# Single-tile node loads in a ring of eight, and more gathered rows fetched by SyncE and ScalarE

## The chip, the cores and the metric

The kernel runs on one core of a Trainium2 chip. The metric is the device time of one execution in microseconds (us); several executions are made and their median is given. The engines are PE (TensorE), DVE (VectorE), ACT (ScalarE), POOL (GpSimd) and SP (SyncE, which only issues transfers here). All run at the same time and wait for each other by semaphores. ACT and SP also have a queue of their own for transfers (ACTq and SPq in the rows).

## The reference

One layer of a graph network over N = 12,500 nodes with D = 256 features and E = 200,000 edges. The edges are sorted by their destination.

```python
h = jnp.maximum(_layernorm(x, axis=-1), 0.0)
agg = jax.ops.segment_sum(h[src], dst, num_segments=N)
z = (1.0 + eps_gin) * h + agg
t = jax.nn.relu(_batchnorm(jnp.dot(z, W1) + b1, g1, bt1))
conv_out = jnp.dot(t, W2) + b2
out = x + jax.nn.relu(_batchnorm(conv_out + h, g2, bt2))
```

The batch norms are over all nodes, so nothing behind the first one can start before t is known for every node.

## The kernel before

**Tiles, groups, windows.** The edges are cut into 1563 tiles of 128. A tile is gathered as 128 rows of 1 KB, one on each partition. Eight tiles make a group; there are 196 groups (the last has three tiles). All edges of a group fall into a window of 96 destination nodes. For each group DVE writes a 0/1 selection matrix, PE multiplies it with the gathered rows (`aggregate`, line 1324, two recorded matmuls a tile), ACT or DVE copies the result out of PSUM (`keep_window`, line 1151, or line 918), PE transposes it (line 1334) and DVE adds it into `aggT` (line 840).

**The x part and the h part.** For groups 0 to 29 the rows of x are gathered, and DVE and ACT compute the layer norm on the gathered rows (`statistics` line 676, `normalise` line 1103). In the same time ACT and DVE normalise the whole of x once, in 25 batches, and store it to HBM as `h_rows`. From group `H_FROM = 30` on the gather reads `h_rows` and no norm is needed.

**Three gatherers.** POOL issues one indirect DMA for a tile (line 650). It takes the groups in order, and a group g waits until group g - 4 has been aggregated (`s_agg`). Some tiles are left out of POOL's list. The last tile of each group in `sp_groups` is fetched by SP, the last but one of each group in `act_groups` by ACT, row by row, each row a DMA of 1 KB whose address comes from a register (lines 512 and 1197). Addresses are brought in as a line of 128 from the HBM table `row_at` (lines 492 and 1178) and read into registers 32 at a time (`reg_load`). Each of the two has three places for tiles (`ROW_BUFS`), so its j-th tile waits for the aggregation of its tile j - 3.

**The pace of SP and ACT.** SP's program goes over passes c = 0 to 97, one for each tile of 128 nodes, thus one pass for two groups. `SP_EIGHTHS` is the number of pieces of 16 rows that it fetches in eight passes: 12, which is 24 rows a pass. ACT's program goes by groups; `ACT_EIGHTHS = 7` is 14 rows a group, from group `H_ACT = 29` on. The lists come out as follows: SP has 16 tiles (two of the x part, groups 16 and 26, and 14 of the h part), ACT has 17 (groups 42 to 188).

**Node tiles.** PE also needs each node tile of h itself, to transpose it (`transpose_h`, line 1351); tile c is transposed in PE's step 2c + 7, where aggregate(g) belongs to step g + 1. The first `H_NODES = 14` are loaded from x and normalised (lines 460 and 1137). The other 84 are loaded from `h_rows` in `quads` of four (line 467), with two quads of space. Quad k >= 2 waits until every tile of quad k - 2 has been transposed, and SP waits there, in the pass with (c - 14) % 4 == 2:

```python
if k >= 2:
    sp.wait_ge(s_hT, H_NODES + QUAD * (k - 1))
```

In every fourth pass SP also stores t to HBM (`store_t`, line 476), for which it waits until four `t` blocks have been made. That is about step 2c.

**ACT around the change of parts.** Up to step 32 ACT's program has, in one step, the norm of the last group, the square roots, then the rows of the step, and behind them `keep_hT`, `keep_window(g - 2)`, `norm_node_tile` and `t_and_b1`. From step 33 on it holds only row fetches until step 191; DVE does the copies.

**The end.** After the last group PE finishes `t`, the first batch norm follows, then the W2 matmuls (line 1442), the second batch norm and the output (line 1456).

Of the kernel before, what the change touches and what calls it, by code (L numbers as in the profile page):

```python
# [20 lines left out]
P = 128  # L21
D = 256
F = 512
DB, FB = D // P, F // P
GT = 8
# [11 lines left out]
XW = Q * D  # L37
X_FIRST = 4
X_EARLY = 16
SP_EIGHTHS = 12  # L40
ACT_EIGHTHS = 7
H_FROM = 30
H_NODES = 14
HB = 4
# [4 lines left out]
ROW_BUFS = 3  # L49
PIECE = 16  # L50
AT_ONCE = 32
QUAD = 4
ROW_BYTES = 4 * D


def ceil(a, b):
    return -(-a // b)


def build(nc, x, src, dst, W1, b1, g1, bt1, W2, b2, g2, bt2, eps_gin, out):  # L60
# [4 lines left out]
    N, E = x.shape[0], src.shape[0]  # L65

    NI = ceil(E, P * SLOTS)
    NT = ceil(N, P)
    assert NI == NT and NI >= 4 and N % 4 == 0 and NI * PG <= BANK
    LASTN = N - P * (NT - 1)  # L70
# [15 lines left out]
    with ctx:  # L86
# [3 lines left out]
        def sem(name):  # L90
            return ctx.enter_context(nc.semaphore(name))
# [4 lines left out]
        h_dram = nc.dram_tensor("h_rows", (N, D), f32, kind="Internal").ap()  # L96
# [3 lines left out]
        def eighths(q, n):  # L100
            return q * n // 8
# [3 lines left out]
        while True:  # L105
            done = ceil(8 * per_tile * (len(sp_groups) + 1), SP_EIGHTHS)
            if done > H_NODES or 2 * (done - 1) + 6 >= H_FROM:
# [3 lines left out]
        while True:  # L111
            done = ceil(8 * per_tile * (len(sp_groups) - SP_X + 1), SP_EIGHTHS) + H_NODES
            if 2 * (done - 1) + 6 >= NG - 4:
# [4 lines left out]
        while True:  # L118
            done = ceil(8 * per_tile * (len(act_groups) + 1), ACT_EIGHTHS) + H_ACT
            if done - 1 + 4 >= NG - 4:  # L120
# [22 lines left out]
        work, once, tables, ring = (arena[:, sum(MAIN[:n]):sum(MAIN[:n + 1])] for n in range(4))  # L143
# [6 lines left out]
                 work[:, 2 * GT * D:3 * GT * D])]  # L150
        hb = [a[:, n * 4 * D:(n + 1) * 4 * D].rearrange("p (j d) -> p j d", d=D) for a in
              (ring[:, 2 * GT * D:3 * GT * D], work[:, 2 * GT * D:3 * GT * D]) for n in (0, 1)]
        quads = [ring[:, 2 * GT * D + n * QUAD * D:2 * GT * D + (n + 1) * QUAD * D].rearrange("p (j d) -> p j d", d=D)
                 for n in (0, 1)]
        assert (NT - H_NODES) % QUAD == 0 and 2 * QUAD == GT
        after_rows = [work[:, 3 * GT * D + n * D:3 * GT * D + (n + 1) * D] for n in range(4)]
        tab_i = [work[:, n * EB * P:(n + 1) * EB * P].bitcast(i32).rearrange("p (b e) -> p b e", e=P) for n in (0, 1)]
        tab_f = [work[:, (2 + n) * EB * P:(3 + n) * EB * P].rearrange("p (b e) -> p b e", e=P) for n in (0, 1)]
# [42 lines left out]
        hx = after_rows[3]  # L201
# [68 lines left out]
        s_bn, s_mv, s_sd, s_rstd, s_st, s_h, s_sel, s_agg, s_add = (  # L270
            sem(n) for n in ("s_bn", "s_mv", "s_sd", "s_rstd", "s_st", "s_h", "s_sel", "s_agg", "s_add"))
        s_xt = [sem("s_xt_even"), sem("s_xt_odd")]
        s_quad = [sem("s_quad_even"), sem("s_quad_odd")]
        s_ev, s_wT = sem("s_ev"), sem("s_wT")
        s_xbn, s_xmv, s_xsd, s_xrs, s_xst, s_hx, s_hT, s_hTc, s_zt, s_t, s_tb, s_tst, s_td = (
            sem(n) for n in ("s_xbn", "s_xmv", "s_xsd", "s_xrs", "s_xst", "s_hx", "s_hT", "s_hTc", "s_zt",
                             "s_t", "s_tb", "s_tst", "s_td"))
# [50 lines left out]
        def row_pieces(first, end, tiles):  # L328

            return [divmod(n, P // PIECE) for n in range(first, min(end, tiles * P // PIECE))]  # L330
# [13 lines left out]
        def batch_nodes(a, b, first, end):  # L344

            return a[b * QN + 4 * first:b * QN + 4 * end, :].rearrange("(p j) d -> p j d", j=4)

        NQUAD = (NT - H_NODES) // QUAD

        def quad_count(k):  # L350

            return 16 * (k // 2 + 1 + (k == NQUAD - 1))

        def quad_tile(c):

            k, j = divmod(c - H_NODES, QUAD)
            return quads[k % 2][:, j, :]

        def wait_h(eng):

            for b in range(NQ - HB, NQ):
                wait_apart(eng, s_hd[b % HB], batch_count(b))
# [49 lines left out]
        def last_order(i):  # L412

            return (NQF, TAILN // 4) if i == 0 else (i - 1, P)
# [13 lines left out]
        def _(sp):  # L428
# [17 lines left out]
            for a in (b1, g1, bt1, b2, g2, bt2):  # L446
                k = a.shape[0] // P
# [7 lines left out]
            def load_node_tile(c, n=P):  # L455
                if c == 1:
                    sp.wait_ge(s_add, 1)
                if c >= 2:
                    sp.wait_ge(s_hx, c - 1)
                sp.dma_start(xt[c % 2][0:n, :], x[bass.ds(c * P, n), :]).then_inc(s_xt[c % 2], 16)  # L460

            def load_quad(k):
                if k >= 2:
                    sp.wait_ge(s_hT, H_NODES + QUAD * (k - 1))
                first = H_NODES + QUAD * k
                n = QUAD if k < NQUAD - 1 else QUAD - 1
                sp.dma_start(quads[k % 2][:, 0:n, :],
                             h_dram[first * P:(first + n) * P, :].rearrange("(j p) d -> p j d", p=P)
                             ).then_inc(s_quad[k % 2], 16)
                if n < QUAD:  # L470
                    sp.dma_start(quad_tile(NT - 1)[0:LASTN, :], h_dram[N - LASTN:N, :]).then_inc(s_quad[k % 2], 16)

            def store_t(q):
                sp.wait_ge(s_tb, FB * (q + 1))
                if q < NQF:
                    sp.dma_start(t_dram[q, :, :, :], tb[:, :, :]).then_inc(s_td if q < NQF - 1 else s_td_full, 16)
                else:
                    sp.dma_start(t_dram[q, :, :, 0:TAILN], tb_last[:, :, :]).then_inc(s_td_tail, 16)
# [11 lines left out]
            def load_at(j):  # L490
                b, p = divmod(sp_groups[j] * GT + GT - 1, P)
                sp.dma_start(sp_at[j % 2], at_dram[b, p:p + 1, :]).then_inc(s_spat[j % 2], 16)
# [26 lines left out]
            def pieces_of_pass(c):  # L519

                if c < H_NODES:
                    return row_pieces(eighths(SP_EIGHTHS, c), eighths(SP_EIGHTHS, c + 1), SP_X)
                c -= H_NODES
                return [(SP_X + j, m) for j, m in row_pieces(eighths(SP_EIGHTHS, c), eighths(SP_EIGHTHS, c + 1),
                                                            len(sp_groups) - SP_X)]

            def load_t(q, k, r, n=QN):
                if at_least(q, 2):
                    sp.wait_ge(s_u, FB * (q - 1))
                sp.dma_start(tin[:, k % 2, :, 0:n],  # L530
                             t_dram[bass.ds(q, 1), :, :, 0:n].rearrange("c p f n -> p (c f) n")
                             ).then_inc(s_tin[k % 2], 16)
# [3 lines left out]
            for c in range(NT):  # L536
                if c == NT - 1:
                    store_t(NQF - 2)
                if c < H_NODES:
                    load_node_tile(c)  # L540
                elif c == H_NODES:
                    wait_h(sp)
                    load_quad(0)
                    load_quad(1)
                elif (c - H_NODES) % QUAD == 2 and (c - H_NODES) // QUAD + 2 < NQUAD + 1:
                    k = (c - H_NODES) // QUAD + 1
                    if k >= 2:
                        load_quad(k)
                if 2 * Q < c < NT - 1 and c % Q == 1:
                    q = (c - 2 * Q - 1) // Q  # L550
                    if q == NQF - 3:
                        sp.wait_ge(s_td, 16 * q)
                        load_t(0, 0, 0)
                    store_t(q)
                if c == 0:
                    sp.wait_ge(s_trc[0], NTR)
                    sp.wait_ge(s_trc[1], NTR)
                    for b in (2, 3):
                        sp.dma_start(hb[b], batch_nodes(x, b, 0, P)).then_inc(s_pl[b], 16)
                    sp.wait_ge(s_atd, 16)  # L560
                    load_at(0)
                for j, m in pieces_of_pass(c):
                    load_rows(j, m)
# [47 lines left out]
            q, n = last_order(NQ - 1)  # L611
# [455 lines left out]
        def _(act):  # L1067
# [136 lines left out]
            def step(g):  # L1204
# [10 lines left out]
                if g >= H_ACT:  # L1215
                    for j, m in row_pieces(eighths(ACT_EIGHTHS, g - H_ACT), eighths(ACT_EIGHTHS, g - H_ACT + 1),
                                           len(act_groups)):
# [72 lines left out]
        def _(pe):  # L1290
# [46 lines left out]
            def transpose_h(c):  # L1337
                n = P if c < NT - 1 else LASTN
                if c < H_NODES:
                    pe.wait_ge(s_hx, c + 1)  # L1340
                else:
                    k = (c - H_NODES) // QUAD
                    pe.wait_ge(s_quad[k % 2], quad_count(k))
                h = hx if c < H_NODES else quad_tile(c)
                if 1 <= c < NT - 1:
                    pe.wait_ge(s_hTc, c)
                if c == NT - 1:
                    pe.wait_ge(s_sel, NG)
                hT = hT_ps if c < NT - 1 else hT_last
                for f in range(DB):  # L1350
                    last = T.transpose(hT[:, f, 0:n], h[0:n, f * P:(f + 1) * P], ident[0:n, 0:n])
                last.then_inc(s_hT, 1)
# [40 lines left out]
            a, c, q = NG - 4, NT - 4, NQF - 2  # L1393
# [90 lines left out]
```

## Time and profile before

| | |
|---|---|
| time, median of 3 runs | 2143.56 us (2143.31 to 2145.06) |
| the profiled execution: time, span | 2143.43 us, 2141.6 us |
| POOL: busy, and indirect DMAs | 1449.2 us (68%), 1530 of them from 3.8 to 1916.5 us |
| PE busy | 1430.6 us (67%) |
| DVE busy, ACT busy | 768.3 us (36%), 338.3 us (16%) |
| rows fetched one by one: SP, ACT | 2048, 2176 |
| HBM read, written | 271.55 MB, 52.05 MB |

The span is from the first to the last recorded instruction. Busy leaves out instructions that only issue a DMA from SP or ACT, register loads and waits. The share of PE is that of pipelined matmuls and is no measure of how near PE is to its limit.

### The profile page before, as it was taken

The numbers are of one execution on the slowest core, as the hardware profiler recorded it, in microseconds if no ns is written. First come the engines' busy times: TensorE is split into PE (matmuls) and PEld (weight loads), VectorE is DVE, ScalarE is ACT, GpSimd is POOL, SyncE is SP. The second block draws the span as 40 slices with busy tenths as digits, with TensorE's granted clock in tenths as the row PEclk, the third lists the DMA queues.
The fourth block names the chain that finished last, engine by engine and source line by source line (L and its number), as shares of the span: only waits on it lengthen the run. The fifth ranks groups of instructions, "written<-read, shape, count | busy, mean of one in ns | idle before, by whom it ended". The sixth has DMA issues, their size and how long they took to land.

```text
span 2141.6 us, 24025 instructions
## 1 busy us (share of the span) xinstructions
PE 1430.6 (67%) x4835; PEld 911.2 (43%) x4835; DVE 768.3 (36%) x1947; ACT 338.3 (16%) x661; POOL 1449.2 (68%) x1540
## 2 busy tenths in 40 slices
PE   3656666665655766675666566666666666689998
PEld 2434344443433434343444334434344444454446
DVE  7777753222322222322232222222232232234447
ACT  6767660000000000000000000000000000014446
POOL 7777777777777777777777777777777777760000
PEclk7788788877888787888888887778787788899999
DMA  6666654444434434444444443443443444448438
GB/s 200 214 224 218 225 175 129 132 117 139 138 108 139 138 110 136 137 118 130 136 126 119 138 139 108 138 137 107 140 137 108 136 135 123 137 133 321 176 135 319
DMA packets 123554, 325.22 MB, mean 152 GB/s; under 512 B 32179, under 2 KB 55294, under 8 KB 117266
## 3 DMA queue, kind: packets, MB, share of 16 engines
q0 software_dynamic: 73440, 200.64, 32.0%
q1 hardware_dynamic: 39100, 97.34, 12.8%
q10 hardware_dynamic: 10870, 25.75, 3.6%
q8 instruction: 38, 0.62, 0.1%
q14 instruction: 106, 0.87, 0.1%
HBM read 271.55 MB, written 52.05 MB: 151 GB/s over the span
## 4 chain that ended last, share of the span: by engine, by line
POOL 65%; issue 21%; PE 12%; DMA 2%; ACT 0%; DVE 0%; SPq 0%; POOLq 0%; DVEq 0%
POOL arena L650 65%; PE ps L1442 8%; PE ps L1324 2%; PE ps L1456 2%; DMA arena<-h_rows,arena 1%; PE ps L1360 0%; PE ps L1398 0%; DMA arena<-in_src 0%; ACT aggT L1072 0%; SPq L439 0%; ACT arena L1078 0%; ACT arena L1076 0%; DVE arena L1057 0%; PE ps L1334 0%; SPq L433 0%
## 5 line engine op out<-in xcount | busy, mean ns | idle before, releaser
L650 POOL DMA_INDIRECT arena<-h_rows,arena x1292 | 1221.6, 946 | 394.0 <-issue 391.5
L1324 PE MATMUL ps<-arena 128*96 128x256 f32 x3060 | 976.9, 489 | 675.2 <-DMA arena<-h_rows,arena 561.5
L1324 PEld LDWEIGHTS ps<-arena 128*96 128x96 f32 x3060 | 640.8, 216 | 993.3 <-issue 732.4
L840 DVE TENSOR_TENSOR aggT<-aggT,ps 128x192 f32 x196 | 69.3, 353 | 1074.2 <-PE ps L1334 1071.2
L1151 ACT COPY arena<-ps 96x256 f32<-96x256 f32 x37 | 13.2, 357 | 1575.5 <-PE ps L1334 1545.0
L650 POOL DMA_INDIRECT arena<-in_x,arena x222 | 209.9, 946 | 67.7 <-issue 67.7
L1360 PE MATMUL ps<-arena 128*128 128x512 f32 (+3 forms) x412 | 186.3, 577 | 1.6 <-DVE arena L873 1.5
L1442 PE MATMUL ps<-arena,W2s 128*128 128x512 f32 (+1 forms) x400 | 168.1, 582 | 0.9 <-ACT arena L1272 0.8
L927 DVE TENSOR_TENSOR arena<-arena,ps 128x768 f32<-128x768 f32 x159 | 149.8, 942 | 0.0
L1103 ACT ACTIVATE arena<-arena,nb,mv 128x256 f32<-128x256 f32 x238 | 120.2, 587 | 83.6 <-DVE nb L744 81.5
L1442 PEld LDWEIGHTS ps<-arena,W2s 128*128 128x128 f32 x400 | 75.7, 190 | 93.2 <-issue 86.3
L676 DVE BATCH_NORM_STATS2 st<-arena 128x6 f32<-128x256 f32 x238 | 80.5, 410 | 61.5 <-DMA arena<-in_x,arena 61.4
L1360 PEld LDWEIGHTS ps<-arena 128*128 128x128 f32 x412 | 69.7, 190 | 48.1 <-issue 44.5
L1272 ACT ACTIVATE arena<-arena,sh,sc 128x512 f32<-128x512 f32 (+1 forms) x100 | 72.1, 792 | 90.2 <-PE ps L1442 80.3
L924 DVE TENSOR_SCALAR arena<-ps,prmT 128x512 f32<-128x512 f32 x79 | 59.3, 751 | 73.7 <-PE ps L1360 73.7
L1035 DVE SCALAR_TENSOR_TENSOR aggT<-ps,prmT,aggT 128x512 f32<-128x512 f32 (+1 forms) x50 | 36.9, 738 | 95.7 <-PE ps L1442 95.7
L881 DVE BATCH_NORM_STATS2 arena<-arena 128x6 f32<-128x512 f32 x92 | 62.9, 684 | 10.3 <-ACT arena L1160 10.3
L1334 PEld LDWEIGHTS ps<-ident,arena 96*128 96x128 f32 x392 | 55.3, 142 | 26.5 <-ACT arena L1151 1.2
L918 DVE COPY arena<-ps 96x256 f32<-96x256 f32 x159 | 65.8, 414 | 0.1
L1334 PE MATMUL ps<-ident,arena 96*128 96x96 f32 x392 | 64.9, 246 | 0.6 <-ACT arena L1151 0.5
L1117 ACT ACTIVATE arena<-arena,pnb,pmv 128x256 f32<-128x256 f32 (+1 forms) x100 | 51.7, 591 | 0.0
L756 DVE TENSOR_TENSOR arena<-arena,ps 128x768 f32<-128x768 f32 x37 | 35.0, 945 | 8.7 <-PE ps L1324 8.7
(99 smaller groups left out, 575.2 us busy)
## 6 DMA issues: line engine op xcount, KB each, us to landing
W2s<-h_rows ACTq DMA_DIRECT2D x2176, 1.0 KB
rl_odd<-h_rows SPq DMA_DIRECT2D x1792, 1.0 KB
t_T<-arena SPq DMA_DIRECT2D x24, 1024.0 KB, 4.9
arena<-t_T SPq DMA_DIRECT2D x24, 1024.0 KB, 4.8
arena<-h_rows,arena POOLq DMA_INDIRECT x1292, 2.8
arena<-in_x SPq DMA_DIRECT2D x27, 512.0 KB, 5.7
h_rows<-arena ACTq DMA_DIRECT2D x24, 512.0 KB, 3.4
out<-arena SPq DMA_DIRECT2D x23, 512.0 KB
```

The costliest lines, as they stand in the source:

```text
L650: nc.gpsimd.indirect_dma_start(out=rows[slot(g)][:, k, :], out_offset=None, in_=(x if g < H_FROM else h_dram)[:, :], in_offset=bass.Indire ...
L676: last = V.bn_stats(o, r)
L840: V.tensor_tensor(z, z, winT_ps, ALU.add).then_inc(s_add, 1)
L881: V.bn_stats(o, t[:, m, :]).then_inc(s_tst, 1)
L918: V.tensor_copy(win_sb[g % 2], win_ps[g % 2]).then_inc(s_ev, 1)
L927: V.tensor_tensor(sel[:, g % 2, :, :], rel[:, g * GT:(g + 1) * GT].unsqueeze(2).to_broadcast([P, GT, W]), iota_ps.unsqueeze(1).to_broadcas ...
L1103: last = S.activation(rows_of(g, k), rows_of(g, k), ACT.Relu, bias=nb[:, g % 2, k:k + 1], scale=mv[:, g % 2, k, 1:2])
L1272: S.activation(u[:, k % 2, f, 0:n], tin[:, k % 2, f, 0:n], ACT.Relu, bias=sh1[:, f:f + 1], scale=sc1[:, f:f + 1]).then_inc(s_u, 1)
L1324: last = T.matmul(win_ps[g % 2], sel[:, g % 2, k, :], rows_of(g, k), start=k == 0, stop=k == n - 1)
L1334: last = T.transpose(winT_ps[:, f, :], win_sb[w % 2][:, f * P:(f + 1) * P], ident[0:W, 0:W])
L1360: last = T.matmul(t_ps[(FB * q + m) % TB][:, a:b], W1s[:, k, m * P:(m + 1) * P], zt[q % 2][:, k, a:b], start=k == 0, stop=k == DB - 1)
L1442: last = T.matmul(c_ps[k % 2][m][:, 0:n], W2s[:, f, m * P:(m + 1) * P], u[:, k % 2, f, 0:n], start=f == 0, stop=f == FB - 1)
```

## The change

The node tiles of the h part are loaded one at a time into a ring of eight places with a semaphore each, in the same memory as the two quads. Four are loaded at pass 14; each later pass c loads tile c + 3, and waits for the transpose of tile c - 5 (`s_hT >= c - 4`). The constants `SP_EIGHTHS` and `ACT_EIGHTHS` go from 12 to 22 and from 7 to 11: 44 rows a pass for SP, 22 a group for ACT. The lists then are: SP 31 tiles (four of the x part, groups 10, 16, 22 and 28, and 27 of the h part), ACT 27 tiles (groups 38 to 190). In 17 groups both fetch a tile (before: in two). The last group of either is 190.

```diff
-SP_EIGHTHS = 12
-ACT_EIGHTHS = 7
+SP_EIGHTHS = 22
+ACT_EIGHTHS = 11
...
-QUAD = 4
+NODE_BUFS = 8
+NODES_AHEAD = 4
...
-            def load_quad(k):
-                if k >= 2:
-                    sp.wait_ge(s_hT, H_NODES + QUAD * (k - 1))
-                first = H_NODES + QUAD * k
-                n = QUAD if k < NQUAD - 1 else QUAD - 1
-                sp.dma_start(quads[k % 2][:, 0:n, :],
-                             h_dram[first * P:(first + n) * P, :].rearrange("(j p) d -> p j d", p=P)
-                             ).then_inc(s_quad[k % 2], 16)
-                if n < QUAD:
-                    sp.dma_start(quad_tile(NT - 1)[0:LASTN, :], h_dram[N - LASTN:N, :]).then_inc(s_quad[k % 2], 16)
+            def load_node_rows(c):
+                n = P if c < NT - 1 else LASTN
+                if c - NODE_BUFS >= H_NODES:
+                    sp.wait_ge(s_hT, c - NODE_BUFS + 1)
+                sp.dma_start(node_tile(c)[0:n, :], h_dram[c * P:c * P + n, :]
+                             ).then_inc(s_node[(c - H_NODES) % NODE_BUFS], 16)
...
                 elif c == H_NODES:
                     wait_h(sp)
-                    load_quad(0)
-                    load_quad(1)
-                elif (c - H_NODES) % QUAD == 2 and (c - H_NODES) // QUAD + 2 < NQUAD + 1:
-                    k = (c - H_NODES) // QUAD + 1
-                    if k >= 2:
-                        load_quad(k)
+                    for n in range(NODES_AHEAD):
+                        load_node_rows(c + n)
+                elif c + NODES_AHEAD - 1 < NT:
+                    load_node_rows(c + NODES_AHEAD - 1)
...
                 else:
-                    k = (c - H_NODES) // QUAD
-                    pe.wait_ge(s_quad[k % 2], quad_count(k))
-                h = hx if c < H_NODES else quad_tile(c)
+                    pe.wait_ge(s_node[(c - H_NODES) % NODE_BUFS], node_count(c))
+                h = hx if c < H_NODES else node_tile(c)
```

## Rows read from the trace of the kernel before

**Rows 1.** The page: busy time of each engine, and 40 slices of POOL

```profile
PE 1430.6 (67%) x4835; PEld 911.2 (43%) x4835; DVE 768.3 (36%) x1947; ACT 338.3 (16%) x661; POOL 1449.2 (68%) x1540
...
POOL 7777777777777777777777777777777777760000
```

**Rows 2.** The page: the chain that ended last, by engine

```profile
POOL 65%; issue 21%; PE 12%; DMA 2%; ACT 0%; DVE 0%; SPq 0%; POOLq 0%; DVEq 0%
```

**Rows 3.** Line 650, POOL's gathers: durations (ns), first and last start, idle time before them

```profile
L650 POOL DMA_INDIRECT arena<-h_rows,arena x1292: 942/946/1005, 302.2 to 1916.5; - x185
L650 POOL DMA_INDIRECT arena<-in_x,arena x222: 942/946/969, 24.6 to 300.9; - x111
...
  issue: 463.7, 1521
  PE ps L1324: 2.4, 8
```

**Rows 4.** Windows of line 650: POOL busy (count), PE's granted clock, DMA share, GB/s

```profile
770.00:800.00 30.00, 22.69 (x25) 0.83 0.37 107
1052.00:1082.00 30.00, 22.69 (x25) 0.83 0.40 116
```

**Rows 5.** Waits: PE's aggregation for gathers (total us, times, longest)

```profile
PE ps L1324 <- DMA arena<-h_rows,arena: 561.5, 150, 7.9
```

**Rows 6.** Timeline of ACT's queue: start us, us

```profile
530.73 0.27 ACTq L1178 DMA_DIRECT2D W2s<-row_at  x1
533.36 51.78 ACTq L1197 DMA_DIRECT2D W2s<-h_rows  x128
585.18 0.27 ACTq L1178 DMA_DIRECT2D W2s<-row_at  x1
```

**Rows 7.** Timeline of SP's queue, h part

```profile
1052.30 30.99 SPq L512 DMA_DIRECT2D rl_odd<-h_rows  x80
1114.06 0.40 SPq L467 DMA_DIRECT2D arena<-h_rows  x1
1114.55 5.12 SPq L512 DMA_DIRECT2D rl_odd<-h_rows  x16
1121.81 0.36 SPq L476 DMA_DIRECT2D t_T<-arena  x1
1122.21 0.27 SPq L492 DMA_DIRECT2D rl_odd<-row_at  x1
1126.68 30.58 SPq L512 DMA_DIRECT2D rl_odd<-h_rows  x80
```

**Rows 8.** DMA queues and issues between 1170 and 1230 us (q10 is ACT's)

```profile
q10 hardware_dynamic: 174, 0.09, 0.6%
...
W2s<-h_rows ACTq DMA_DIRECT2D x83, 1.0 KB
```

**Rows 9.** x part: SP's row fetches, a node tile's issue, and DVE's reading it

```profile
61.95 14.53 SPq L512 DMA_DIRECT2D rl_odd<-in_x  x32
...
97.32 11.87 SPq L512 DMA_DIRECT2D rl_odd<-in_x  x32
114.77 0.37 SPq L460 DMA_DIRECT2D arena<-in_x  x1
...
139.70 0.41 DVE L676 BATCH_NORM_STATS2 xst<-arena 128x6 f32<-128x256 f32 x1
```

**Rows 10.** Timeline of ACT and PE at the change of parts

```profile
308.63 4.04 ACT L1103 ACTIVATE arena<-arena,nb,mv 128x256 f32<-128x256 f32 x8 [6.40 <-DVE nb L744]
...
312.68 0.35 ACT L1151 COPY arena<-ps 96x256 f32<-96x256 f32 x1
...
313.99 0.23 ACTq L1178 DMA_DIRECT2D W2s<-row_at  x1
...
316.63 0.49 ACTq L1197 DMA_DIRECT2D W2s<-h_rows  x1
...
318.15 3.67 PE L1324 MATMUL ps<-arena 128*96 128x256 f32 x16
```

More of the change, by code:

```diff
@@ L152, in build @@
               (ring[:, 2 * GT * D:3 * GT * D], work[:, 2 * GT * D:3 * GT * D]) for n in (0, 1)]
-        quads = [ring[:, 2 * GT * D + n * QUAD * D:2 * GT * D + (n + 1) * QUAD * D].rearrange("p (j d) -> p j d", d=D)
-                 for n in (0, 1)]
-        assert (NT - H_NODES) % QUAD == 0 and 2 * QUAD == GT
+        node_rows = ring[:, 2 * GT * D:3 * GT * D].rearrange("p (j d) -> p j d", d=D)
+        assert NODE_BUFS == GT
         after_rows = [work[:, 3 * GT * D + n * D:3 * GT * D + (n + 1) * D] for n in range(4)]
@@ L272, in build @@
         s_xt = [sem("s_xt_even"), sem("s_xt_odd")]
-        s_quad = [sem("s_quad_even"), sem("s_quad_odd")]
+        s_node = [sem(f"s_node{b}") for b in range(NODE_BUFS)]
         s_ev, s_wT = sem("s_ev"), sem("s_wT")
@@ L346, in batch_nodes, with node_tile, node_count @@
             return a[b * QN + 4 * first:b * QN + 4 * end, :].rearrange("(p j) d -> p j d", j=4)
[L348 to L357, printed above, removed]
+        def node_tile(c):
+            return node_rows[:, (c - H_NODES) % NODE_BUFS, :]
+        def node_count(c):
+            return 16 * ((c - H_NODES) // NODE_BUFS + 1)
         def wait_h(eng):
```

## The prediction

> **What bounds the kernel now.** I read the page first. No engine is busy above 68%, but POOL's slices stand at 7, without a dip, for nine tenths of the span [rows 1]. The chain that ended last gives POOL 65%, "issue" 21% and PE 12% [rows 2]. So I read the line of the gathers next. Each takes 946 ns. The h part's 1292 start between 302.2 and 1916.5 us, so one comes every (1916.5 - 302.2) / 1291 = 1.2504 us. The 0.304 us between two of them (463.7 / 1521) is POOL's own issue time, for it waits for PE only 2.4 us in total [rows 3]. The reader should see that a busy share of 76% here is a full engine. The waits say the same from the other side: PE waits 561.5 us for gathers in 150 places [rows 5]. From 3.8 to 1916.5 us the time is the number of POOL's gathers times 1.2504 us. Behind that lie 225 us (2141.6 - 1916.5) of PE-led work that the change doesn't touch.
>
> **What the change removes.** SP has 31 tiles instead of 16, ACT 27 instead of 17. POOL's list falls by 15 + 10 = 25 gathers, from 1530 to 1505, and 25 x 1.2504 = 31.3 us go, if nothing else becomes late. What could become late is taken in turn: the two row queues, the x part, the change of parts, PE, and the DMA engines.
>
> **ACT's queue, 22 rows a group.** A tile fetched back to back takes 54.45 us from one `row_at` load to the next (530.73 to 585.18), reads of registers and the load within it [rows 6]. In that stretch SP fetched rows as well, for a part of it. After the change a group has 8 - 44/128 = 7.656 POOL tiles, so it lasts 9.573 us, and ACT owes a tile every 128/22 = 5.82 groups, or 55.7 us. It is 98% full, but it fits. It also has a start: its first tile can be complete at about 309 + 54 = 363 us, while group 38 is gathered by POOL at about 387 us. Each tile adds 1.2 us to these 24 us. Its wait for a free place (`s_agg` of its tile three earlier) isn't reached with that lead.
>
> **SP's queue, 44 rows a pass.** SP is paced by `store_t` in every fourth pass, so I sum a round of four passes, which is eight groups or 76.6 us. It has 176 rows. Sixteen rows take 5.12 us, so a row costs 0.32 us; 80 rows take 30.58 us, so each of the two reads of 32 registers in them costs (30.58 - 25.6) / 2 = 2.5 us [rows 7]. 176 x 0.32 = 56.3; 5.5 reads x 2.5 = 13.7; the read behind the store of t takes 4.2 us (1122.48 to 1126.68), 1.7 more than the others; four node loads of 0.40 us and 0.1 us to the next issue are 2.0; the store 0.4; 1.4 loads of addresses 0.4. The sum is 74.5 us, 97% of the round. The other streams don't slow it: 80 rows took 30.99 and 30.58 us beside ACT's.
>
> The smaller node loads are paid here: four issues instead of one in a round, 3 x 0.5 = 1.5 us of the sum. The new wait on `s_hT` is for the transpose in step 2c - 3. The old one held SP until step 2c + 1 in its pass. `store_t` holds SP until step 2c, so I expect the new wait to hold nothing. So the ring by itself is worth nothing, in either direction; with the old waits a round of 74.5 us would fit as well, since they too come once in four passes. What lies behind SP's waits is its row tiles and node tiles. The last pass of a round, c + 3, ends at about step 2c + 7.6, and what it finished is used in step 2(c + 3) + 7, so 5.4 groups or 52 us are spare. Costs that SP hides fall on nobody until these are gone.
>
> **The x part.** SP has 32 pieces in the first 12 passes instead of 16 in 11. Here 32 rows take 11.87 to 14.53 us, dearer than in the h part [rows 9]; a pass of three pieces is about 20 to 22 us, against 19.6 us for two groups. SP drifts by some us, and no piece is left for passes 12 and 13. What is queued behind them is the next node tile. Before, that of pass 4 was issued at 114.77 us, and DVE read it at 139.70 us [rows 9]. From pass 1 at 61.5 us on, three passes of three pieces put pass 4 at about 128 us. With some 3 us to land that leaves 8 us, the least of all passes by this count. I take nothing for the x part; its bound is what passes each 3 us longer would cost, 1 to 2 us. Two of the 25 gathers are saved in it.
>
> **The change of parts.** In steps 29 to 32 ACT has five pieces instead of three, ahead of the window copies that PE waits for. Before, step 29 had none: norm at 308.63 us, window copy at 312.68 us; step 30 began its rows 2.6 us behind the `row_at` load at 313.99 us (316.63) [rows 10]. Everything is 2.5 us earlier by now. In step 29 the load, the read of registers and 16 rows take about 8 us from 306.2 us, of which the norm's 4.04 us cover half. So the copy slips by 4 us, and so does the aggregation that began at 318.15 us and ended at 321.8 us [rows 10]. POOL needs it for group 33, 24 gathers behind the start at 302.2 us, at 332.2 us. Its spare time falls from 10.4 to 6.4 us. In step 31 there are 32 rows and a read, 13.5 us, and the copy comes 10 us later than before. That aggregation ends at about 339 us, while POOL needs it at about 350 us. No loss; bounds are nothing, and 10 us if each of the five pieces took twice its 5.1 us and a read.
>
> **PE.** A group lasted (8 - 26/128) x 1.2504 = 9.75 us, and PE waited 561.5 / 162 = 3.5 us of it, so its own work is 6.3 us. It gets 9.57 us, and in the groups where both SP and ACT fetch a tile 7.5 us. It fits, with four groups of buffer.
>
> **The DMA engines.** No byte is added. POOL made 25 gathers in 30 us both beside ACT's rows alone and beside ACT's and SP's; the DMA share was 0.37 and 0.40 [rows 4]. The row packets themselves: ACT's queue had 0.6% of 16 engines for 60 us, 5.8 us for 83 rows, 0.07 us a row [rows 8]. In a group 44 rows are 3.1 us. If all fell on one engine, that one would be busy 0.37 x 9.57 + 3.1 = 6.6 us of 9.57 us.
>
> The Trainium skill speaks against such rows. "DMA: Bandwidth & Descriptors", section "Why a DMA increments its semaphore by 16 and not by 1", says that a transfer whose slowest dimension doesn't divide further runs on few engines, the lowest-numbered of the 16. No row here shows the engine of a packet. By that rule the sum would be the same, as long as this one engine isn't full. The section "Issuing engines are not separate DMA queues" says that issuing from several engines saves only issue time; issue time is what the gathers of rows 3 are made of, so there the trace agrees.
>
> **The sum.** 2143.43 - 31.3 = 2112.2 us against the profiled execution, 0.13 us below the median: 2112.3 us.
>
> **The rivals.**
> - *Stall at the change of parts or in the x part.* For it: both ACT and SP hold copies and node tiles behind rows there. Against it: 6 and 8 us of spare time. 2 to 10 us, thus 2114 to 2122 us. Chance 0.06.
> - *A row queue is late (the slower side).* ACT and SP have never been full together for more than 31 us. If ACT needed more than (1841.5 - 363) / 26 = 56.9 us a tile, its last one would be later than POOL's group 190 (1885.2 - 35 x 1.25 = 1841.5 us). At 58.1 us, 7% above 54.45, the 31.3 us are lost; at 60 us its last tile is 82 us late and the time about 2194 us, slower than before. SP decides from a round of 76.6 + (52 + 31) / 19.6 = 80.8 us, 8% above its sum. Against it: the tile of rows 6 and the 80 rows of rows 7 were fetched at full pace, with the other queue at work for part of the time. Chance 0.06, half of it above 2148 us.
> - *PE becomes the bound.* It would need half as much work again for each group; 2120 to 2143 us. Chance 0.03.
> - *One DMA engine fills up with rows.* From 0.138 us a row, twice the measured one, a group would last as long as that engine; at three times it would be 3.5 + 9.3 = 12.8 us, and 162 groups of the h part would add some 520 us. Chance 0.02.
> - *The forecast:* 0.83.
>
> **How the numbers follow.** The forecast's own spread is that of the three runs, 1.8 us. From 2110.5 us the range reaches over the nearer half of the stalls, to 2119 us. About 4.3 us (0.2%) is what can be told from no change. Faster: 0.83 + 0.06 + 0.03 + 0.03 less a little, 0.93; same 0.02; slower 0.05.
>
> **What would show it.** Right: line 650 has 1505 starts, 1.250 us apart, the last at about 1885 us, with PE as releaser for under 5 us in total; ACT's `row_at` loads are 54 to 55 us apart throughout; SP's round holds 176 rows in about 74 us and its line for the node load shows no wait; the part behind the last gather is still 225 us. Wrong: gaps in line 650 around 300 to 350 us with PE as releaser (first rival), or late in the h part, with PE waiting for DMA into `rl_odd` or `W2s` (second).

## The result and the profile after

The changed kernel takes 2169.32 us (median of 4 runs, 2166.32 to 2170.07) against 2143.43 us: ratio 1.0117, 95% interval 1.0099 to 1.0134. By the medians it is 25.9 us slower. The forecast was 2112.3 us, 2110.5 to 2119 us, with a chance of 0.05 for slower.

The page of the changed kernel, its busy times, POOL's 40 slices and the chain that ended last:

```profile
PE 1369.2 (63%) x4835; PEld 883.3 (41%) x4835; DVE 766.2 (35%) x1947; ACT 338.4 (16%) x661; POOL 1425.5 (66%) x1515
...
POOL 7777777777777777777767767677666777760000
...
POOL 40%; SPq 24%; issue 18%; PE 13%; DMA 5%; ACT 0%; DVE 0%; POOLq 0%; DVEq 0%
```

Beside [rows 1] and [rows 2], the reader should see two things. POOL's slices now have sixes from the middle of the h part on. And a quarter of the chain is SP's queue, which before was nowhere in it. The line of the gathers (line 641 now) answers to [rows 3]:

```profile
L641 POOL DMA_INDIRECT arena<-h_rows,arena x1269: 940/946/962, 299.8 to 1940.7; - x182
...
  issue: 453.9, 1488
  PE ps L1315: 60.2, 16
```

There are 1505 gathers in all, as forecast, and each still takes 946 ns. But POOL waited for PE for 60.2 us, and the last one starts at 1940.7 us. Counted over all steps between gathers, 56.3 us are above 1.2504 us a step (0.9 us before, near the start, and about the same there now). This excess is called POOL's loss below. The account closes: 2141.6 - 31.3 (25 gathers) + 55.4 (new stalls) + 1.9 (the part behind the last gather is 227.0 us instead of 225.1) = 2167.6, and the span is 2167.7 us. So the 31.3 us were saved, and a new wait took more than that back.

Whom PE and DVE wait for, in the changed kernel (total us, times, longest):

```profile
DVE arena L915 <- DMA t_T<-arena: 283.1, 15, 34.9
PE ps L1315 <- DMA rl_odd<-h_rows: 172.0, 14, 21.9
PE ps L1315 <- DVE arena L918: 92.0, 8, 24.0
...
POOL arena L641 <- PE ps L1315: 60.2, 16, 9.8
```

None of the first three was there before. `rl_odd` holds SP's row tiles, `t_T` is SP's store of t. Both come from SP: it is late. The third follows from the first: DVE can't write the next block of t until the store is done, the selection matrix (line 918) comes behind that, and PE needs the matrix. SP's own waits between 330 and 1860 us say so, of the kernel before and of the changed one:

```profile
SPq L467 <- PE ps L1351: 630.7, 19, 64.0
SPq L476 <- DVE arena L924: 126.5, 20, 20.2
```

```profile
SPq L498 <- PE ps L1315: 11.2, 6, 3.2
SPq L469 <- DVE arena L915: 2.7, 2, 1.6
```

Before, SP waited 757 us of 1530 us in these two lines (`store_t` and the quads' wait). Now it waits 14 us. It has next to no spare time, where the forecast had left it 3%. Its queue in one round, from a store of t to the next:

```profile
1008.09 0.42 SPq L469 DMA_DIRECT2D t_T<-arena  x1
1008.55 0.85 SPq L485 DMA_DIRECT2D rl_odd<-row_at  x1
1013.03 23.50 SPq L505 DMA_DIRECT2D rl_odd<-h_rows  x48
1036.58 0.37 SPq L463 DMA_DIRECT2D arena<-h_rows  x1
1037.04 13.56 SPq L505 DMA_DIRECT2D rl_odd<-h_rows  x32
1050.65 0.36 SPq L463 DMA_DIRECT2D arena<-h_rows  x1
1051.11 18.93 SPq L505 DMA_DIRECT2D rl_odd<-h_rows  x48
...
1073.06 21.14 SPq L505 DMA_DIRECT2D rl_odd<-h_rows  x48
1094.25 0.37 SPq L463 DMA_DIRECT2D arena<-h_rows  x1
1094.67 0.44 SPq L469 DMA_DIRECT2D t_T<-arena  x1
```

The round is 1094.67 - 1008.09 = 86.6 us for 176 rows; the mean of 15 rounds is 83.2 us. By [rows 7] 48 rows with one read of registers would be 17.9 us. Here they are 18.9 to 23.5 us. From one row of SP to the next it takes 0.377 us in the mean instead of 0.332 us (420 to 1600 us, steps over 1.5 us, thus the reads of registers, left out). The median is 0.322 us in both kernels: most rows cost what they did, and some cost much more. In the 15 rounds of the changed kernel 185 of 2525 steps are over 0.5 us (22 of 1380 in 15 rounds before). They are densest behind a store of t: the mean step is 0.45 us in the first 20 us behind one and 0.36 us in the rest of the round.

One stall, in the chain between 940 and 1000 us:

```profile
951.52 0.23 SPq L505
952.16 19.29 DMA rl_odd<-h_rows
971.46 0.24 issue
971.70 6.00 PE ps L1315 x16
977.70 0.26 issue
977.96 0.94 POOL arena L641
```

PE and POOL in the timeline of the same stretch:

```profile
971.70 5.13 PE L1315 MATMUL ps<-arena 128*96 128x256 f32 x12 [11.61 <-DMA rl_odd<-h_rows]
977.96 0.94 POOL L641 DMA_INDIRECT arena<-h_rows,arena  x1 [5.58 <-PE ps L1315]
```

A row issued at 952.16 us lands 19.3 us later. PE waits 11.61 us for it, POOL waits for PE, and the gather that should start at 972.7 us starts at 977.96 us. In the h part there are 14 such gaps over 0.1 us in POOL's gathers, together 55.4 us; this is the first. SP's lead was nearly used up by then.

### The profile page after: what moved, and what is told of

Its sections match the earlier page's. It is cut to its first block, busy times and chain, and to the rows that moved or that the text cites. A ratio compares the mean times of both kernels' runs of the same rounds, so it can differ in the third digit from the quotient of the medians.

```text
span 2167.7 us, 30622 instructions
## 1 busy us (share of the span) xinstructions
PE 1369.2 (63%) x4835; PEld 883.3 (41%) x4835; DVE 766.2 (35%) x1947; ACT 338.4 (16%) x661; POOL 1425.5 (66%) x1515
## 4 chain that ended last, share of the span: by engine, by line
POOL 40%; SPq 24%; issue 18%; PE 13%; DMA 5%; ACT 0%; DVE 0%; POOLq 0%; DVEq 0%
POOL arena L641 40%; SPq L505 19%; PE ps L1432 8%; SPq L498 4%; PE ps L1315 3%; DMA rl_odd<-h_rows 3%; DMA arena<-h_rows,arena 2%; PE ps L1446 1%; PE ps L1350 1%; SPq L463 0%; PE ps L1388 0%; DMA arena<-in_src 0%; SPq L469 0%; SPq L436 0%; ACT aggT L1063 0%
## 5 line engine op out<-in xcount | busy, mean ns | idle before, releaser
L641 POOL DMA_INDIRECT arena<-h_rows,arena x1269 | 1199.7, 945 | 442.5 <-issue 382.2
L1315 PE MATMUL ps<-arena 128*96 128x256 f32 x3010 | 910.0, 469 | 761.0 <-DMA arena<-h_rows,arena 313.6
L1315 PEld LDWEIGHTS ps<-arena 128*96 128x96 f32 x3010 | 604.0, 206 | 1041.9 <-issue 800.7
L918 DVE TENSOR_TENSOR arena<-arena,ps 128x768 f32<-128x768 f32 x159 | 149.7, 942 | 0.0
L1094 ACT ACTIVATE arena<-arena,nb,mv 128x256 f32<-128x256 f32 x236 | 119.2, 587 | 80.8 <-DVE nb L735 80.8
L1341 PE MATMUL ps<-ident,arena 128*128 128x128 f32 x196 | 37.3, 273 | 2.3 <-ACT aggT L1135 2.3
```

Of the source, the lines that this page charges most:

```text
L641: nc.gpsimd.indirect_dma_start(out=rows[slot(g)][:, k, :], out_offset=None, in_=(x if g < H_FROM else h_dram)[:, :], in_offset=bass.Indire ...
L918: V.tensor_tensor(sel[:, g % 2, :, :], rel[:, g * GT:(g + 1) * GT].unsqueeze(2).to_broadcast([P, GT, W]), iota_ps.unsqueeze(1).to_broadcas ...
L1094: last = S.activation(rows_of(g, k), rows_of(g, k), ACT.Relu, bias=nb[:, g % 2, k:k + 1], scale=mv[:, g % 2, k, 1:2])
L1315: last = T.matmul(win_ps[g % 2], sel[:, g % 2, k, :], rows_of(g, k), start=k == 0, stop=k == n - 1)
```

## The experiments

All are edits of the changed kernel, where nothing else is said. The ratio is to the kernel before, run on the same chip; there it took 2143.6 to 2143.9 us, but 2148.2 us beside e5 to e8, and far more beside the four runs at the end of this section.

**Parts of the change.** Theory A was that the two row queues share a path which is nearly full at 44 rows a group; theories B and C put the blame on the ring or on SP by itself.

Ring alone (e1), and new rates with the old quads (e2, an edit of the kernel before):

```diff
-SP_EIGHTHS = 22
-ACT_EIGHTHS = 11
+SP_EIGHTHS = 12
+ACT_EIGHTHS = 7
```

```diff
-SP_EIGHTHS = 12
-ACT_EIGHTHS = 7
+SP_EIGHTHS = 22
+ACT_EIGHTHS = 11
```

> The ring of eight places alone, with the old rates (24 rows a pass, 14 a group). Theory A (row fetches of the two queues share one path that is nearly full at 44 rows a group; a backlog of some 12 us stands in it): node loads of one tile change nothing, 2143 us within 2 us, and a node load lands after 2 to 5 us. Theory B (the single node loads and the waits of the ring disturb SP): above 2150 us.

Measured: 2144.56 us, ratio 1.0005 (0.9995 to 1.0015).

> The old quads with the new rates (44 rows a pass, 22 a group). Theory A: as slow as the changed kernel or slower, 2165 to 2185 us, since the rates fill the path and SP is late in the same way. Theory B: SP keeps up once the node loads are gone, 2112 to 2120 us.

Measured: 2159.74 us, ratio 1.0076 (1.0059 to 1.0093); POOL lost 47.6 us, SP's rounds are 82.4 us. Theory B falls: the ring changes nothing at the old rates, and without it the new rates are slow as well. The time is below the range that I had written down. Where SP is full, the ring costs some 10 us more; three more issues a round point that way, but nothing isolates it.

One queue at a time (e3: `ACT_EIGHTHS = 7`; e4: `SP_EIGHTHS = 12`):

> The changed kernel with ACT back at 14 rows a group; SP stays at 44 rows a pass. 15 gathers fewer than before are 18.8 us. Theory A (shared path; the whole demand is 36 rows a group instead of 44): SP keeps its round of about 75 us, 2124.7 us within 3 us, and a node load lands within 5 us. Theory C (SP alone can't issue 176 rows in 76.6 us, whatever ACT does): SP's round stays at 81 to 84 us and the time at 2155 us or more.

Measured: 2128.07 us, ratio 0.9929 (0.9912 to 0.9945), rounds of 76.7 us, POOL lost 1.5 us, node loads land after 4.6 us in the median. The time is 0.4 us above the range of theory A; 2.0 us of it lie behind the last gather (227.1 us instead of 225.1).

> The changed kernel with SP back at 24 rows a pass; ACT stays at 22 rows a group. 10 gathers fewer than before are 12.5 us. Theories A and C both: ACT keeps up with a tile in 54 to 55 us, 2130.9 us within 3 us. If ACT can't hold its pace by itself: above 2140 us.

Measured: 2131.41 us, ratio 0.9946 (0.9929 to 0.9962). Either half of the new rates makes the kernel faster, near the count of gathers saved; both together make it slower. SP's rounds shrink from 83.2 to 76.7 us when ACT fetches less, and nothing of SP's own program has changed. Theory C falls.

**What the shared path is.** The node loads show a backlog. Line 463, first in the changed kernel, then in e1: what an issue takes in ns, and in the last line issue to landing in us:

```profile
L463 SPq DMA_DIRECT2D arena<-h_rows x84: 327/365/1342, 292.3 to 1896.5; - x84
...
DMA to landing us min/median/max: 2.1/19.9/22.8
```

```profile
L463 SPq DMA_DIRECT2D arena<-h_rows x84: 327/366/1344, 293.1 to 1824.6; - x84
...
DMA to landing us min/median/max: 2.1/3.1/5.7
```

The same transfer lands 3.1 us after its issue with few rows and 19.9 us with many (medians). The start of each packet tells where it waits. A store of t has 128 packets of 8 KB. Worked out from the packets' records, the us from issue to start:

```
kernel, store at        median    93%    95%    last
before, 1047.7 us          2.2    3.5    3.6     3.7
changed, 1094.7 us         2.3    3.4   18.4    21.2
changed, 1343.2 us         3.3    4.5   22.1    24.9
e2, 1091.6 us              2.8    4.0   15.0    18.4
e3, 1035.0 us              2.4    3.7    3.7     4.0
```

In the changed kernel and in e2, 15 of 16 shares (93.75%) start within 5 us, and one sixteenth, 8 packets, waits 15 to 25 us. A packet's record doesn't name its engine, but the reading is that one of the 16 DMA engines has a queue before it and the others have none. ACT's 1 KB packets, matched in order to its rows, start 11.3 us after their row's issue (1.6 us before). The Trainium skill says in "DMA: Bandwidth & Descriptors", section "Why a DMA increments its semaphore by 16 and not by 1", that a transfer issued by SP or ACT uses as many engines, up to 16, as divide its slowest dimension, and always the lowest-numbered ones: 16 for 128 partitions, and a single one where nothing divides. The trace agrees: a row is one packet, a store of 128 partitions has 8 packets in each share, and the share that waits is one. Which engine it is, no record shows.

The queue builds up slowly, and it is what makes a row dear. In the changed kernel ACT's delay is 1.3 us at 316 us, 5.9 us at 390 us and 10.5 us at 450 us. While it is below 8 us, the mean step from one row of SP to the next is 0.335 us (reads of registers left out, steps under 2.3 us); from 8 to 14 us of delay it is 0.375 to 0.394 us.

**Moving load off that engine.** Theory D says the engine's time for row packets is the limit, theory E the making of the transfers. In e5 to e7 each row is given as 2, 4 and 16 parts:

```diff
-sp.dma_start(sp_rows[j % ROW_BUFS][e:e + 1, :].bitcast(mybir.dt.uint8),
-             a[bass.ds(at, ROW_BYTES)].rearrange("(p e) -> p e", p=1)
+sp.dma_start(sp_rows[j % ROW_BUFS][e:e + 1, :].bitcast(mybir.dt.uint8).rearrange("p (k e) -> p k e", k=2),
+             a[bass.ds(at, ROW_BYTES)].rearrange("(p k e) -> p k e", p=1, k=2)
```

> The changed kernel; each row that SP or ACT fetches is moved as two parts of 512 bytes in the same DMA. Theory D (the full path is one DMA engine that every row packet falls on; two parts go to two engines): the backlog falls from 12 us to a few, SP's round fits in 76.6 us and the time goes toward 2112 to 2130 us. Theory E (the full path is the making of descriptors for the two queues, or a number of descriptors in flight): twice the descriptors, the backlog stays or grows, 2169 us or more.

> As e5, with four parts of 256 bytes. Theory D: no backlog if the smaller packets cost the engine less than a whole one; 2112 to 2130 us, unless issuing a row becomes dearer than 0.33 us. Theory E: slower again than e5.

> As e5, with sixteen parts of 64 bytes. Theory D: the load is spread over all engines, but packets this small may cost nearly as much as one of 1 KB; the backlog is small if they cost less than 50 ns each. Theory E: much slower, above 2250 us.

Measured: ratios 1.0100 (1.0083 to 1.0117) and 1.0104 (1.0087 to 1.0121), and 2169.76 us in one run of e7. ACT's queue has about as many packets between 420 and 1600 us as in the changed kernel (5517): 5469 in e5, 5509 in e6 and 5507 in e7. So parts that adjoin in memory were moved as one packet; the three are the changed kernel once more and tell nothing of D and E.

e9 and e10 keep the parts apart in the tile's memory, for both queues, e11 with four parts for ACT alone:

```diff
-        act_rows = [w2_early[:, b * D:(b + 1) * D] for b in range(ROW_BUFS)]
+        act_parts = w2_early[:, 0:ROW_BUFS * D].rearrange("p (k b e) -> p k b e", k=PARTS, b=ROW_BUFS)
+        act_rows = [act_parts[:, :, b, :] for b in range(ROW_BUFS)]
```

> The changed kernel; a row that SP or ACT fetches in the h part goes to two places that don't adjoin in the tile's memory, as two parts of 512 bytes, so that they can't be merged. In e5 to e7 the parts adjoined and were moved as one packet. SP's first h tile waits for its last x tile, some 15 us later than before. Theory D (one DMA engine takes all row packets and is full): each of two engines has half the bytes; the backlog falls below 5 us, SP's round to 77 us, 2112 to 2125 us. Theory E (making of descriptors is full): 2170 us or more.

> As e9 with four parts of 256 bytes. Theory D: the backlog is gone, and the time is 2112 to 2120 us unless issuing a row is dearer than the 0.33 us of one part. Theory E: slower than e9.

> Four parts for ACT's rows alone; SP's rows stay whole. Theory D: the engine keeps SP's 22 rows a group and a quarter of the bytes of ACT's 22; the backlog is small, 2112 to 2125 us. Theory E: as slow as e10.

Measured: ratios 1.6619 (1.6592 to 1.6647) and 1.6596 (1.6569 to 1.6624), and 3267.97 us in one run of e11. The parts were separate now (6912 packets of 512 bytes on ACT's queue for its 3456 rows in e9), but another cost came in. SP's issue of an h row in e9 (durations in ns):

```profile
L514 SPq DMA_DIRECT2D rl_odd<-h_rows x3456: 2/606/1577, 316.9 to 3281.1; - x192
```

It takes 606 ns in the median where a whole row takes 228, and a row comes every 0.73 us. Two parts and four cost the same (606 and 607 ns). The range of theory D was missed because of this price, so the three don't tell D from E; they close this way around the engine.

e12 and e16 halve the bytes and leave the form. SP's part is shown, ACT's is alike from its fourth tile on; the second half of each row isn't fetched:

```diff
-                    sp.dma_start(sp_rows[j % ROW_BUFS][e:e + 1, :].bitcast(mybir.dt.uint8),
-                                 a[bass.ds(at, ROW_BYTES)].rearrange("(p e) -> p e", p=1)
+                    n = D if j < SP_X else D // 2
+                    sp.dma_start(sp_rows[j % ROW_BUFS][e:e + 1, 0:n].bitcast(mybir.dt.uint8),
+                                 a[bass.ds(at, 4 * n)].rearrange("(p e) -> p e", p=1)
```

> The changed kernel, with only the first 512 bytes of each row fetched by SP (in the h part) and by ACT (from its fourth tile on); the other half of these rows is left out and the product uses what the place held. Number and form of the DMAs are the same. Theory D (one engine's time per packet): a packet takes about 30 ns instead of 46 where it isn't disturbed, the backlog falls from 12 us to below 6, SP's round from 82.6 us to 77, ratio 0.985 to 0.996. Theory E (issue, descriptors): ratio 1.010 to 1.013.

Measured: ratio 0.9991 (0.9980 to 1.0001), between the two ranges. POOL lost 28.2 us instead of 56.3, and the rounds are 81.1 us instead of 83.2. But the backlog, which theory D wanted below 6 us, didn't shrink: ACT's delay is 12.6 us (11.3 us in the changed kernel), and a node load lands after 20.8 us in the median (19.9 us). And the two queues together get hardly further. Rows issued per us between 450 and 1600 us:

```
kernel          SP     ACT    both
changed        2.11   2.32    4.43
e2             2.13   2.32    4.45
e16            2.16   2.29    4.45
```

With half the bytes the sum is the same within 0.4%. SP, which was the late one, got a little more of it and ACT a little less, and that is what the time shows; why the shares moved isn't known. A packet of ACT takes 27 ns in the median instead of 46, and 74 ns in the mean instead of 95 (62 ns in the kernel before), so the recorded time of the row packets isn't what fills the engine either. Theory D as it was written fails: the queue stands before one engine, but halving the bytes doesn't empty it. Theory E doesn't explain why 15 of 16 shares of a store pass at once. What a row costs that engine beyond its bytes stays open.

**From which demand it is full.** The demand is SP's rows a group (half of those a pass) plus ACT's 22, 20, 18 or 14. e8: `SP_EIGHTHS = 20`, `ACT_EIGHTHS = 10`; e17: 22 and 9; e18: 20 and 11.

> The changed kernel with 40 rows a group (SP 40 a pass, ACT 20 a group): 18 gathers fewer than before are 22.5 us. If the path is full only above some 40 rows a group: 2121 us within 3 us, a backlog of 4 to 8 us. If it is full below: 2130 us or more, with PE waiting for SP's rows.

> SP 44 rows a pass, ACT 18 a group: 40 rows a group and 20 gathers fewer than before, 25.0 us. If only the sum of both queues counts, as e8 with 40 rows a group was free of stalls: ratio 0.9883 (2118.5 us), SP's round 76.6 us. If SP's own 176 rows a round are too many beside that: ratio above 0.992.

> SP 40 rows a pass, ACT 22 a group: 42 rows a group and 21 gathers fewer, 26.3 us. If the path is full between 42 and 44 rows a group: ratio 0.9877 (2117.3 us). If between 40 and 42: ratio above 0.992, PE waits for SP's rows.

Measured: 2125.82, 2120.62 and 2118.72 us. The time of e8 is outside its range of 2121 us within 3 us, but it ran where the kernel before took 2148.2 us, and its ratio is the forecast one. With the other kernels in order of demand: "Count" is the ratio by the gathers saved alone; the delay is from an ACT row's issue to its packet's start, its mean between 420 and 1600 us; SP's row is the mean step of 0.377 us from above. It has the single node loads in it wherever the ring is, so 0.340 us of e1 is the level without a backlog there.

```
kernel   rows a group   saved   count    ratio (95%)                 delay   SP's row  round
before   12 + 14 = 26     0     1.0000   1                            1.6 us  0.332 us  78.0 us
e1       12 + 14 = 26     0     1.0000   1.0005 (0.9995 to 1.0015)    1.6     0.340     78.1
e4       12 + 22 = 34    10     0.9942   0.9946 (0.9929 to 0.9962)    1.9     0.339     77.4
e3       22 + 14 = 36    15     0.9912   0.9929 (0.9912 to 0.9945)    4.3     0.343     76.7
e8       20 + 20 = 40    18     0.9895   0.9894 (0.9878 to 0.9911)    7.1     0.345     76.6
e17      22 + 18 = 40    20     0.9883   0.9889 (0.9872 to 0.9905)    6.5     0.349     76.5
e18      20 + 22 = 42    21     0.9877   0.9882 (0.9866 to 0.9899)   10.2     0.359     77.1
changed  22 + 22 = 44    25     0.9854   1.0117 (1.0099 to 1.0134)   11.3     0.377     83.2
```

The ratios follow the count up to 42 rows a group. The backlog is there from 36 on and costs next to nothing by itself, since each tile and node tile has a lead of some groups. What costs is that the rows don't get through: at 44 rows SP needs 83 us for a round of 76.6 us. 44 rows in 9.57 us would be 4.60 a us, and 4.43 to 4.45 were issued wherever that was asked for; e18 asks for 4.38 and gets 4.39. By this estimate the limit lies near 42.5 rows a group. In e17 SP fetches the same 176 rows a round and keeps its time, as ACT fetches less. e18 beats both kernels, with 2118.72 us. Its gathers and the landing of its node loads:

```profile
L641 POOL DMA_INDIRECT arena<-h_rows,arena x1272: 942/946/962, 301.2 to 1890.6; - x182
```

```profile
L463 SPq DMA_DIRECT2D arena<-h_rows x84: 328/366/2359, 292.4 to 1806.9; - x84
...
DMA to landing us min/median/max: 4.5/19.1/22.7
```

The last gather starts at 1890.6 us, and POOL lost 1.2 us, although a node load lands as late as in the changed kernel. By the rate it stands close to the edge.

**Runs that tell nothing here.** Four kernels ran where the kernel before itself took 2614 us: e12 (ratio 1.2238), and three rates, of which two were repeated as e17 and e18.

> The changed kernel, with only the first 512 bytes of each row fetched by SP (in the h part) and by ACT (from its fourth tile on); the other half of these rows is left out and the product uses what the place held. Number and form of the DMAs are the same. Theory D (one engine's time per packet): a packet takes about 30 ns instead of 46, the backlog falls from 12 us to below 6, SP's round from 82.6 us to 77, time 2112 to 2135 us. Theory E (issue, descriptors): 2165 to 2172 us.

> SP 44 rows a pass, ACT 18 a group: 40 rows a group and 20 gathers fewer than before, 25.0 us. If only the sum of both queues counts, as e8 with 40 rows a group was free of stalls: ratio 0.9883 (2118.5 us), SP's round 76.6 us. If SP's own 176 rows a round are too many beside that: ratio above 0.992.

> SP 40 rows a pass, ACT 22 a group: 42 rows a group and 21 gathers fewer, 26.3 us. If the path is full between 42 and 44 rows a group: ratio 0.9877 (2117.3 us). If between 40 and 42: ratio above 0.992, PE waits for SP's rows.

> The old quads with SP 40 rows a pass and ACT 20 a group, as e8 but for the ring: 18 gathers fewer, 22.5 us. If the ring is worth nothing where the path isn't full: ratio 0.9895, within 0.1% of e8's 0.9894. If the quads' waits hold SP back: ratio above 0.992.

Ratios of e13 to e15: 1.2117, 1.1697 and 1.1533. POOL had 124 to 130 steps of over 1.6 us between two gathers in each of them (one in the trace of the kernel before), and single pieces of rows took twice their time. The cause isn't known, so these figures aren't compared with the rest. Whether quads would do as well as the ring at 40 rows a group stays open with them.

## Why the prediction was wrong

- **POOL bounds the kernel, 1.2504 us a gather.** Right. 25 gathers were worth 31.3 us, and e4, e8, e17 and e18 give what their count says within their intervals.
- **SP's queue: "so a row costs 0.32 us", "The other streams don't slow it".** This step failed. The 0.32 us came from 16 rows behind a long wait, and the second 80 rows of [rows 7] followed 30 us of rest too, but for 16 rows. Kept up with both queues full, a row costs 0.379 us to the next one (where nothing but the next row follows, over the 15 rounds). 176 x 0.059 = 10.4 us more, 84.9 us for the round, against 83.2 us measured. The sum of 74.5 us was right for a lighter load: in e3 the same 176 rows took rounds of 76.7 us, of which SP waited some 1.8 us for others. I had taken the price of a row as fixed, whatever the two queues do, on the ground that [rows 7]'s 80 rows ran "beside ACT's". That reading was too strong: ACT fetched from 1064.27 us on, during 19 of the 31 us, and from 1152.36 us on, during the last 5 us of the second 80 rows.
- **The one DMA engine.** I worked out 6.6 us of 9.57 us for the worst case and gave the rival 0.02. That is where the reason lies, by the shares of the stores. The 0.07 us of [rows 8] was the recorded time of ACT's packets in a queue that was mostly idle. For a row packet alone it is 0.062 us before and 0.095 us in the changed kernel, still below the rival's 0.138 us; e16 shows that this time isn't the engine's price. From the rate of 4.43 rows a us one row passes every 0.226 us, all other traffic included. The 31 us in which both queues were busy couldn't show the limit. In such a stretch of the kernel before (507 to 538 us, where SP's 80 rows took 30.53 us) ACT's delay rose to 4.0 us at most and fell again; in the changed kernel it took some 100 us to pass 8 us, where the rows get dearer.
- **The rival "a row queue is late".** It named the right victim and the right sign: it put the loss of the whole gain at a round of 80.8 us; the measured rounds are 83.2 us. By its formula they would cost 6.6 x 19.6 - 52 = 77 us, and 55.4 us were lost. It had half of 0.06 for a time above 2148 us.
- **ACT's queue.** Right: 54.8 us from one load of addresses to the next here (524.74 to 579.50), 52.9 to 56.5 us in all but the first and the last, and PE never waits for a row of ACT.

```profile
472.82 51.88 ACTq L1188 DMA_DIRECT2D W2s<-h_rows  x128
524.74 0.30 ACTq L1169 DMA_DIRECT2D W2s<-row_at  x1
527.40 52.07 ACTq L1188 DMA_DIRECT2D W2s<-h_rows  x128
579.50 0.27 ACTq L1169 DMA_DIRECT2D W2s<-row_at  x1
```

- **The ring by itself is worth nothing.** Right (e1) at the old rates. At the new ones the kernel with the ring is 9.6 us slower than e2.
- **PE.** It isn't the bound, as forecast: in the stall shown it starts late and doesn't run long.
- **The x part and the change of parts: no loss.** Right. By the prediction's shifts the norm that began at 313.97 us would begin at 315.5 us (2.5 us earlier, 4 us later), and the copy that 32 rows hold up, at 327.44 us before, at 334.9 us (2.5 us earlier, 10 us later). They began at 316.19 and 334.93 us, and POOL's first new gap is at 972.7 us. The changed kernel, ACT:

```profile
316.19 0.60 ACT L1094 ACTIVATE arena<-arena,nb,mv 128x256 f32<-128x256 f32 x1 [0.44 <-DVE nb L735]
...
323.90 10.93 ACTq L1188 DMA_DIRECT2D W2s<-h_rows  x32
334.93 0.37 ACT L1142 COPY arena<-ps 96x256 f32<-96x256 f32 x1 [12.65 <-issue]
```

- **The stalls.** SP's lead of 52 us lasted until about the first stall: its eight rounds from 349.9 to 1008.1 us took 658.2 us, 45 us more than 8 x 76.6. POOL then lost 55.4 us in 14 places, between 972 and 1641 us.

## What to carry to other kernels

Work that is moved from a full engine to idle queues meets a price that rises with their load. Take it from a stretch in which the queue runs as long and as full as it will after the change, and not from a burst behind a wait; if there is none, try half of the move first. Look at the time from issue to landing of the other transfers in the same queue: it rose from 3 to 20 us here, while the mean share of the 16 DMA engines was 0.44 before and 0.45 after (420 to 1600 us). And a queue that is 97% full by a sum of its best prices has room only as long as these prices hold: it kept up in e3 and e17, and not with four more rows a group from its neighbour.

## What was not expected of the hardware

- Transfers of one row from both queues wait in one queue, by all signs that of one DMA engine of 16. When 44 rows of 1 KB are asked for in 9.6 us beside the gathers, its backlog is 11 us, and the other 15 shares of a store start within 5 us; the mean share of the 16 engines is 0.43 between 1022 and 1129 us.
- Rows of 512 bytes get through hardly faster than rows of 1 KB: 4.45 and 4.43 a us.
- With this backlog issuing itself becomes dearer, from 0.33 to 0.38 us a row in the mean. The median stays at 0.322 us; it is single issues that take over 0.5 us.
- A row in two or four parts that don't adjoin takes 606 ns to issue instead of 228 (e9 and e10).
